# Projected rows of a graph attention block: scaled out of PSUM by ScalarE and added to x by GpSimd, in place of VectorE

## What is computed

```python
def _L0_gnn_ref(node_features, adjacency_matrix, W, b_W, a_vec, b_a):
    h = node_features @ W.T + b_W
    a1, a2 = (a_vec[:D_OUT], a_vec[D_OUT:])
    e = (h @ a1)[:, None] + (h @ a2)[None, :] + b_a[0]
    e = jnp.where(e > 0, e, 0.2 * e)
    scores = jnp.where(adjacency_matrix > 0, e, jnp.float32(NEG_INF))
    attention = jax.nn.softmax(scores, axis=1)
    return attention @ h
...
x = x + _L0_gnn_ref(_layernorm(x, axis=-1), adj, L0_gnn_W, L0_gnn_b_W, L0_gnn_a_vec, L0_gnn_b_a)
x = x + _L0_ffn_ref(_layernorm(x, axis=-1)[None], L0_ffn_gate_w, L0_ffn_gate_b, L0_ffn_w1, L0_ffn_w2, L0_ffn_w3)[0]
```

## Time and profile before

| what | value |
|---|---|
| median of 3 runs | 1891.75 us (1890.79 to 1894.92) |
| the profiled execution: its own time | 1883.58 us |
| its span, first to last instruction | 1881.8 us |
| mean granted TensorE clock | 0.95 of full speed |
| busy in the span: PE, DVE, ACT, POOL | 1535.9, 1470.3, 1278.7, 604.0 us |
| main loop | about 240 to 1470 us for the host blocks 1 and up |

### The profile page before, as it was taken

One profiled execution on the slowest core, in us unless ns is written; L12 is line 12 of the kernel. 1 busy time (PEld: TensorE's weight loads), 2 busy tenths in 40 slices (PEclk: granted clock), 3 DMA queues, 4 the chain that ended last, 5 costly groups with the idle time before them and its releaser, 6 DMA issues.

```text
span 1881.8 us, 24594 instructions
## 1 busy us (share of the span) xinstructions
PE 1535.9 (82%) x8112; PEld 854.9 (45%) x8113; DVE 1470.3 (78%) x2024; ACT 1278.7 (68%) x1620; POOL 604.0 (32%) x840
## 2 busy tenths in 40 slices
PE   5587899898899889889988988899995058888880
PEld 5454444454454445434444543455553035555560
DVE  7799999999989999998999899889874113433344
ACT  4899899698779878887987888677563024444440
POOL 6500012221341225133213604222325634444450
PEclk9999999999999999999999999999998569999995
DMA  6899687487748757764876676454231142222229
GB/s 196 300 319 320 199 273 243 137 265 238 222 145 277 226 160 249 241 223 138 270 233 189 211 247 222 126 162 146 66 113 44 35 135 64 61 62 59 65 59 271
DMA packets 143075, 339.40 MB, mean 180 GB/s; under 512 B 16962, under 2 KB 64258, under 8 KB 142978
## 3 DMA queue, kind: packets, MB, share of 16 engines
q1 hardware_dynamic: 120784, 303.26, 51.1%
q0 software_dynamic: 11824, 28.50, 4.7%
q10 hardware_dynamic: 10370, 6.38, 1.1%
HBM read 309.57 MB, written 28.51 MB: 180 GB/s over the span
## 4 chain that ended last, share of the span: by engine, by line
PE 34%; DVE 32%; issue 17%; POOL 8%; ACT 5%; DMA 3%; SPq 0%; ACTq 0%; DVEq 0%; POOLq 0%
DVE probs L1196 15%; PE pair L898 15%; DVE ring L1142 13%; PE pair L985 7%; PE pair L885 4%; PE pair L1001 4%; ACT ring L690 3%; PE pair L992 2%; DMA ring<-res_d 1%; POOL xd_d L604 1%; ACT probs L741 1%; POOL ln L565 1%; PE pair L981 1%; POOL numT L574 1%; POOL xd_d L657 1%
## 5 line engine op out<-in xcount | busy, mean ns | idle before, releaser
L898 PE MATMUL pair<-probs,X 128*128 128x512 f32 x2048 | 1013.9, 613 | 1.8 <-ACT probs L741 1.6
L741 ACT ACTIVATE probs<-probs,ebias 128x1024 f32<-128x1024 f32 (+1 forms) x576 | 602.4, 1047 | 264.4 <-DVE probs L1196 263.1
L1196 DVE SCALAR_TENSOR_TENSOR probs<-s1row,ns,pair 128x1024 f32<-128x1024 f32 (+1 forms) x576 | 658.2, 1157 | 65.8 <-PE pair L885 63.6
L1142 DVE CUSTOM_DVE_ANT_0 ring<-urow,ring 128x2048 int8<-128x2048 f16 x256 | 596.4, 2331 | 10.1 <-ACT ring L690 10.0
L690 ACT ACTIVATE ring<-stage,neghalf 128x1024 int8<-128x1024 int32 x512 | 574.8, 1140 | 1.3 <-DMA stage<-in_adj 0.9
L885 PEld LDWEIGHTS pair<-diag,ring 128*128 128x128 fp8e5 x4096 | 266.0, 99 | 485.3 <-DVE probs L1196 254.7
L898 PEld LDWEIGHTS pair<-probs,X 128*128 128x128 f32 x2048 | 347.3, 192 | 220.5 <-issue 215.7
L885 PE MATMUL pair<-diag,ring 128*128 128x128 bf16 x4096 | 327.2, 221 | 147.0 <-DVE probs L1196 120.9
L1417 DVE COPY probs<-pair 128x256 f32<-128x256 f32 x144 | 61.2, 425 | 188.4 <-PE pair L992 180.3
L985 PE MATMUL pair<-ring,probs 128*128 x288 | 167.7, 666 | 42.1 <-issue 41.2
L662 POOL DMA_INDIRECT res_d<-probs x144 | 139.2, 966 | 181.9 <-ACT probs L789 178.2
(11 more groups left out here) (217 smaller groups left out, 839.1 us busy)
## 6 DMA issues: line engine op xcount, KB each, us to landing
stage<-in_adj SPq DMA_DIRECT2D x512, 512.0 KB, 4.3
probs<-xd_d SPq DMA_DIRECT2D x144, 65.0 KB, 1.8
ring<-res_d SPq DMA_DIRECT2D x16, 512.0 KB, 8.7
ring<-in_L_ffn_w SPq DMA_DIRECT2D x2, 2048.0 KB, 12.6
out<-ring ACTq DMA_DIRECT2D x8, 512.0 KB, 7.3
xres<-in_x POOLq DMA_DIRECT2D x7, 512.0 KB, 7.5
s1row<-s_d SPq DMA_DIRECT2D x7, 512.0 KB, 6.8
xmid_d<-xres POOLq DMA_DIRECT2D x7, 512.0 KB, 5.8
```

Source lines behind the costliest of these rows:

```text
L741: act.activation(probs[:, n % PR, 0:wide], probs[:, n % PR, 0:wide], ACT.Exp, bias=ebias[:, j:j + 1], scale=RISE).then_inc(probs_ready, 1)
L898: m = pe.matmul(acc[q][:, lo:hi], X[:, j, :], probs[:, n % PR, lo:hi], start=(j == 0), stop=(j == NT - 1))
L1142: dve.tensor_tensor_reduce(m, urow[:, c * CH:(c + 1) * CH], m, CODE, NO_EDGE, ALU.subtract, ALU.max, part[:, k, c:c + 1]).then_inc(piece_d ...
L1196: dve.scalar_tensor_tensor(out=probs[:, n % PR, 0:wide], in0=s1row[:, q, 0:wide], scalar=ns2[:, j:j + 1], in1=Tp[n % 2][:, 0:wide], op0=AL ...
```

## The change

For the blocks 0 to 6 (`by_act`: b < NB - 2), VectorE keeps the denominators, the reciprocals and the gate columns of a round and no longer does the rows. It gives a new semaphore, den_ready, with the gate columns. ScalarE scales each row tile out of PSUM into numT, one instruction to a step, at steps 15 to 18 and 28 to 31 of the host block and behind that step's exponential and signs, and gives proj_read with the last of a round. GpSimd waits for x and adds numT to it with one more instruction, before it overwrites numT with the share. Blocks 7 and 8 stay as they were.

```diff
@@ -375,6 +376,10 @@
+        def by_act(b):
+
+            return b < NB - 2
+
@@ -536,6 +541,9 @@
                 pool.wait_ge(proj_read, ROUND0[b + 1])
                 share = numT[:, 0:n * D].rearrange("p (k d) -> p k d", d=D)
                 rows = xres[:, q, 0:n, 0:D]
+                if by_act(b):
+                    pool.wait_ge(xres_in[q], 16 * (b // 2 + 1))
+                    plink(pool.tensor_tensor(rows, rows, share, ALU.add))
                 pool.tensor_tensor(share, mean_row[:, 0:D].unsqueeze(1).to_broadcast([P, n, D]),
@@ -751,6 +759,17 @@
+            def scaled_rows(b, r, i):
+
+                q, k = b % 2, 4 * r + i
+                at = k % 4 // 2 * 512 + k % 2 * GW
+                if i == 0:
+                    act.wait_ge(den_ready, ROUND0[b] + r + 1)
+                ins = act.activation(numT[:, k * P:(k + 1) * P], acc[q][:, at:at + D], ACT.Copy,
+                                     scale=rden[:, k:k + 1])
+                if k == min(4 * r + 4, BLOCKS[b]) - 1:
+                    ins.then_inc(proj_read, 1)
+
@@ -763,6 +782,11 @@
                     if j == 5 and b >= 1:
                         numerators(b - 1)
+                    if b >= 1 and by_act(b - 1):
+                        for r in range(ROUNDS[b - 1]):
+                            i = j - (11 + 13 * r + 4)
+                            if 0 <= i < min(4, BLOCKS[b - 1] - 4 * r):
+                                scaled_rows(b - 1, r, i)
@@ -1228,10 +1252,14 @@
                     dve.tensor_tensor(nshare[:, w], noedge[:, w], rden[:, w], ALU.mult)
-                    dve.tensor_tensor(pgs[:, w, :].rearrange("p (h c) e -> p h c e", c=2), four[:, :, :, D + 1:GW],
-                                      pairs(rden).unsqueeze(3).to_broadcast([P, (tiles + 1) // 2, 2, E]), ALU.mult)
-                    dve.wait_ge(xres_in[q], 16 * (b // 2 + 1))
-                else:
+                    ins = dve.tensor_tensor(pgs[:, w, :].rearrange("p (h c) e -> p h c e", c=2),
+                                            four[:, :, :, D + 1:GW],
+                                            pairs(rden).unsqueeze(3).to_broadcast([P, (tiles + 1) // 2, 2, E]), ALU.mult)
+                    if by_act(b):
+                        ins.then_inc(den_ready, 1)
+                    else:
+                        dve.wait_ge(xres_in[q], 16 * (b // 2 + 1))
+                elif not by_act(b):
                     k = 4 * r + step - 4
                     at = k % 4 // 2 * 512 + k % 2 * GW
                     ins = dve.scalar_tensor_tensor(out=xres[:, q, k, 0:D], in0=acc[q][:, at:at + D],
```

More of the change, by code:

```diff
@@ L321, in graph_moe_layer @@
         fin = sem("fin")
+        den_ready = sem("den_ready")
         proj_read = sem("proj_read")
```

## The result

The changed kernel takes 1886.12 us (median; 1881.86 to 1890.52, 9 runs), the kernel before beside it 1894.92 us (1890.79 to 1900.71, 9 runs). The ratio is 0.9954, with a 95% interval of 0.9938 to 0.9970: 8.8 us or 0.46% faster, between 5.7 and 11.7 us. The forecast was 6.2 us faster and 1885.6 us. The profiled execution of the changed kernel took 1888.3 us, with a span of 1886.5.

A forecast was written before the change was run, and what follows sets the result against it. VectorE was taken to bound host blocks 1 to 6, TensorE host block 7. Five blocks at 2.08 - 1.0 = 1.08 us plus 0.8 in host block 1 made 6.2 us: 1891.75 - 6.2 = 1885.6 us, range 1883.5 to 1888.

The forecast's parts named there:

- VectorE sets the pace of host blocks 1 to 6: Middle host block: VectorE works 160.1 of 167.5 us, TensorE 149.9, so VectorE bounds blocks 1 to 6.
- A row costs 0.26 us on the path: Each row instruction leaving VectorE saves 0.26 us; eight save 2.08 us a block, 44 save 11.4 us.
- ScalarE's rows cost nothing: Steps 15 to 18 and 28 to 31: 1.1 us a round fits in ScalarE's idle time, so no cost.
- The rival of a ScalarE bound: Steps 15 to 18 and 28 to 31: ScalarE becomes the bound, 1896 to 1909 us; chance 0.12.
- The order behind the second round: Arrival times of GpSimd's three operations and VectorE's ring instructions, steps 33 to 36; two ring instructions wait, 1.0 and 1.8 us.
- Its price: Behind the second round: 2.8 us of held-up ring instructions against 1.81 before, 1.0 us more a block.
- Host block 1: One round of four rows saves 1.04 us, some 0.2 of a ring instruction is held up: 0.8 us gained.
- Host block 7: TensorE works 132.3 of 133.0 us and bounds it, so its eight removed rows gain nothing.
- The sum: Five host blocks at 1.08 give 5.4 us, host block 1 gives 0.8, host block 7 nothing: 6.2 us.
- The lock takes all: Rival: each added GpSimd addition holds up a ring instruction for its whole length; 1892.5 us, no change; chance 0.25.
- The base: Whole kernel: the median before, 1891.75 us, from which the forecast subtracts 6.2 us.
- What was predicted of the profile: L1237 x12, 52 ScalarE rows near 370 ns, long ring instructions of about 3.2 and 4.1 us, blocks of 166.4 us.

The follow-up runs named there:

- Experiment 4: Changed kernel without GpSimd's added addition, so x is left out of the rows of blocks 0 to 6: 1870.68 us, ratio 0.9909.
- experiment 5: Kernel before plus one small unread ScalarE activation at each of the change's 52 places, rows staying on VectorE: 1897.07 us beside 1893.33.
- experiment 11: Kernel before plus three small unread ScalarE activations at each of the change's 52 places, rows staying on VectorE: 1900.20 us beside 1899.59.
- experiment 1: Kernel before, unedited, run once more for a second profile: 1888.89 us.
- experiment 2: Changed kernel, unedited, run once more on the same chip as the kernel before: 1879.79 us against 1888.89.
- Experiments 7 and 12: Changed kernel with GpSimd's three operations a block cut in halves, one set per round, run twice: 1871.20 us; 1868.07 us, ratio 0.9892.
- 8: Changed kernel with GpSimd's three operations halved, three halves also waiting for a ring instruction to be done: 1874.57 us, ratio 0.9900.
- experiment 6: Kernel before with GpSimd's share product and last addition halved, one pair per round, rows staying on VectorE: 1882.76 us, ratio 0.9938.
- 9: Kernel before, unedited, run a third time in another group: 1893.19 us, one execution.
- experiment 10: Changed kernel, unedited, run a third time beside the kernel before: 1895.03 us against 1893.19, one execution each.

## Why the prediction was right

The direction and the range held, and the mechanism was the one forecast, instruction by instruction. Taking the terms of the sum:

- **VectorE sets the pace of host blocks 1 to 6: right.** 56.01 of 56.08 us.
- **A row costs 0.26 us on the path: right.** Experiment 4 takes 2.08 us a block through the rows, once the 1.31 of the ring instruction are set apart.
- **ScalarE's rows cost nothing: right**, by experiment 5, though the reckoning behind it was far too narrow. It read the idle time at two instructions, while the stretch has eight waits with 8.2 us. That the slack is the sum over these waits is argued from experiment 11, in which 8 x 1.16 = 9.3 us of added work cost 0.21 us. The rival of a ScalarE bound, at 1909, got a chance of 0.12 by that error; it needed more than three times the added work.
- **The order behind the second round: right at each meeting.** The prediction had the eighth row at 458.1, ring 33 at 457.89, ring 34 at 461.3, the last addition at 466.4, ring 36 at 466.8 and the statistics at 470.8. In the profile they are at 462.69 (462.33 + 0.36), 462.48, 465.89, 470.79, 471.28 and 475.06. The host block began 5.6 us later (first logits 380.2 against 374.6) and the first round gave 1.04 of it back, so 4.6 lie between the two reckonings: 462.7, 462.5, 465.9, 471.0, 471.4 and 475.4.
- **Its price: this is the term that was mis-sized.** "2.8 us of held-up ring against 1.81 now" was 2.34 against 1.81. Both meetings came out some 0.2 too large: 0.78 for 1.0 and 1.56 for 1.8. The GpSimd operations ended 0.1 to 0.2 us earlier than I had added up, and a held-up ring instruction runs on about 0.1 us before the recorded end of the GpSimd operation: before, it began with 1.95 us of the addition still to go and lost 1.81. I had seen that difference and called it "almost exactly". So the net gain of a block was 1.5 us where 1.08 stood: five blocks are 7.6 us instead of 5.4.
- **Host block 1:** 161.1 to 159.95 us, 1.15 where 0.8 was forecast. Up to step 36 it is 0.85, the 1.04 of the rows less the 0.18 by which one ring instruction was held up (2.46 us), as forecast; the other 0.3 lies at step 51, where VectorE sat idle 0.21 us in front of the logits before and doesn't now. This term was missing. **Host block 7:** nothing forecast, 0.5 us lost in experiments 1 and 2 (the first logits of the last block move by 8.7 us, those of host block 7 by 9.3). The meeting there grew as well, from a ring instruction of 2.81 us to one of 4.05 to 4.07 in all three executions; TensorE's bound hides it only in part.
- **The sum:** 7.6 + 1.15 - 0.5 is 8.25. Of the 9.1 between experiments 1 and 2 another 0.5 comes from host block 0 and 0.4 from behind the last logits. The change does nothing in either place, and the second differs by 2 us between executions of the kernel before (445.24 to 447.26), so they are taken as chance. The medians gave 8.8, the forecast 6.2.
- **"The lock takes all", at 1892.5:** its worst order of arrival didn't come. The Trainium skill's rule (SBUF — State Buffer, section "SBUF: two separate sides"), by which of GpSimd and a VectorE instruction with two SBUF inputs the first to start has the shared pair of ports for the whole instruction and the other stands still, is borne out by every meeting above: the one that came second ended about one length after the one that came first.
- **The base:** the forecast compared with a median of three runs, 1891.75, and nine runs gave 1894.92; with that base the same sum would have said 1888.7. That the forecast's 1885.6 lies within 0.5 us of the measured 1886.12 is luck: a base 3.2 us too low and a gain 2.6 us too small cancel. The 8.8 are a difference, and so are not touched by it.

What was predicted of the profile: L1237 x12 (L1265 x12), rows near 370 ns (351), two long ring instructions a block of about 3.2 and 4.1 (3.07 and 3.85), a block of 166.4 (166.0, and 167.0 in the profiled execution, by the wait at step 3), statistics that don't wait (475.06, right behind the ring instruction).

What stays open is host block 0. The first logits of host block 1 start between 216.0 and 221.2 us. Part of that goes with the granted clock. In experiment 2 TensorE's clock was at its upper level of 2.4 GHz, then for 10.24 us at the lower, 1.2 GHz, then up again; TensorE had worked 7.94 of the 10.20 us before it fell:

```profile
117.20:127.40 10.20, 7.94 (x50) 5.31 (x50) 10.20 (x14) 9.73 (x12) 0.00 (x0) 1.00 0.96 347
127.40:137.64 10.24, 9.76 (x35) 6.47 (x36) 8.00 (x10) 9.98 (x12) 0.00 (x0) 0.50 0.98 335
```

VectorE works 8.00 of those 10.24 us instead of all of them, and the stretch from step 15 to 36 of host block 0 is 42.83 us, 2.45 longer than in experiment 1 (40.38). The three executions of the changed kernel and experiment 4 have such a fall of 10.2 us between steps 15 and 36 of host block 0, and the 42.83; the three of the kernel before have falls of 6.8 us at most and 40.38. Experiments 7 and 12, with falls of 6.8 us, lie between (41.44, 41.23), and 8, without one, has 40.38 with the same rows on ScalarE. Experiments 6 and 11, in which the rows stay on VectorE, have falls of 10.2 us too (in 6 it begins before step 15), with 41.73 and 41.82. So such a fall needs no moved row. Whether the changed code, which does nothing in that block, makes it longer or more frequent, I couldn't settle.

## What to carry to other kernels

When two engines exclude each other by instruction, cost a moved operation by writing out who arrives when, on both engines, up to the point where they part again; its length says little (0.47, 1.9 and about 0 us were paid for the same 1.9 to 2.2 us of work). Cut the operations of the engine that has time until each fits into the gaps of the one that hasn't: this was worth more (10.9 us on top of the change, by the two comparisons, and 10.6 us alone) than moving the rows (8.8 us), and waits that place them by hand brought nothing on top that the times show. And read the slack of an engine over a whole stretch, not at the one wait beside the edit.

## What was not expected of the hardware

- Of two dependent GpSimd operations 0.08 us apart (466.81 to 466.89), a waiting ring instruction got in between, in every meeting shown here: a chain of three long operations doesn't keep the ports for 6 us, and each of them can both wait and be waited for.
- The stretches from 15 to 59 of the full host blocks repeat to 0.04 us within an execution and between chips (with one exception, the 54.60 us in experiment 6). What differs between executions and chips is host block 0 (5 us) and the logits of step 3 (0 to 2.6 us a block, once 4.0). The times of two single executions can hide an effect of 1.5 us a block, as 9 and 10 do; the stretches show it in them.
- The wait at step 3 differs by group, from 0.94 to 3.54 us with the same code (once, in experiment 10, 4.9). Its releaser is mostly given as TensorE's transposes, but those are shown at their usual place. What the engines really waited for isn't in the profile.
